# Two row buffers and one scaled-value buffer in decayed attention, and half of the last sums on VectorE

## What is computed

```python
# second layer's attention, 16 query heads, 4 K,V heads, head width 64
q, k, v = x @ Wq.T, x @ Wk.T, x @ Wv.T          # split into heads
q, k = rope(q), rope(k)                          # x * cos + rotate_half(x) * sin
k, v = repeat(k, 4), repeat(v, 4)
# per head with slope s, causal, no softmax:
out[t] = sum over u <= t of exp(-s * (t - u)) * (q[t] . k[u]) * v[u]
x = layernorm(x + out @ Wo.T)
# end of the second layer's feed-forward: every token has two expert answers
x = layernorm(2 * x + answer0 + answer1)         # the kernel's form of it, factors folded in
```

## Time and profile before

| what | value |
|---|---|
| median of 3 runs | 3228.32 us (3227.73 to 3229.99) |
| the profiled execution | 3231.17 us, its span 3229.4 us |
| PE busy | 2767.0 us (86%) |
| DVE busy | 1985.2 us (61%) |
| ACT busy | 1299.3 us (40%) |
| POOL busy | 1068.6 us (33%) |
| granted TensorE clock, mean | 0.942 of full |

### The profile page before, as it was taken

The page is one execution under the profiler, slowest core; times in us unless marked ns, Lnnn a source line. Parts: engine busy times, 40 slices in busy tenths (PEclk is TensorE's granted clock), DMA queues, the critical chain, the costliest instruction groups (busy, mean ns, idle before and its releaser), DMA issues. The chain is left out here.

```text
span 3229.4 us, 62896 instructions
## 1 busy us (share of the span) xinstructions
PE 2767.0 (86%) x17098; PEld 1956.6 (61%) x17099; DVE 1985.2 (61%) x3659; ACT 1299.3 (40%) x2735; POOL 1068.6 (33%) x1446
## 2 busy tenths in 40 slices
PE   6998989999898978877999999969999999809992
PEld 4666666666675647765666666644555555408992
DVE  3656666565666658864555555557777777546664
ACT  2554554545454532212222222215555555424443
POOL 4333343434334311115555555510111111122225
PEclk8999999999999989999999999979999999959996
DMA  2111011111101121112111110022222222052225
GB/s 64 34 31 41 28 38 41 27 38 27 44 24 38 34 80 33 39 70 72 33 32 32 32 32 26 26 67 75 70 65 63 64 64 64 18 172 87 72 74 199
DMA packets 146409, 175.43 MB, mean 54 GB/s; under 512 B 21130, under 2 KB 109730, under 8 KB 145570
## 3 DMA queue, kind: packets, MB, share of 16 engines
q1 hardware_dynamic: 135076, 149.89, 15.9%
q0 software_dynamic: 6912, 18.96, 1.6%
q10 hardware_dynamic: 4224, 4.19, 0.4%
HBM read 90.83 MB, written 37.06 MB: 40 GB/s over the span
## 5 line engine op out<-in xcount | busy, mean ns | idle before, releaser
L560 ACT ACTIVATE soft_probs<-soft_ps_s,soft_mx 128x512 f32<-128x512 f32 x512 | 347.8, 685 | 395.1 <-DVE soft_mx L479 370.4
L479 DVE TENSOR_REDUCE soft_mx<-soft_ps_s 128x1 f32<-128x512 f32 x512 | 329.4, 685 | 236.7 <-PE soft_ps_s L389 224.1
L1817 DVE TENSOR_REDUCE mla_mx<-mla_ps_s 128x1 f32<-128x512 f32 x512 | 334.9, 686 | 133.7 <-PE mla_ps_s L1670 133.2
L1928 ACT ACTIVATE mla_pt<-mla_ps_t 128x512 f32<-128x512 f32 x512 | 289.9, 596 | 265.2 <-PE mla_ps_t L1682 263.1
L389 PE MATMUL soft_ps_s<-soft_ks,soft_qs 128*128 128x512 f32 x1024 | 309.8, 422 | 13.9 <-ACT soft_probs L560 13.9
L398 PE MATMUL soft_ps_p<-ident,soft_probs 128*128 128x128 f32 x2048 | 266.4, 273 | 12.0 <-DVE soft_mx L479 8.5
L398 PEld LDWEIGHTS soft_ps_p<-ident,soft_probs 128*128 128x128 f32 x2048 | 236.7, 141 | 46.7 <-DVE soft_mx L479 10.6
L489 DVE COPY soft_pt<-soft_ps_p 128x512 f32<-128x512 f32 x256 | 175.6, 686 | 138.7 <-PE soft_ps_p L398 134.0
L389 PEld LDWEIGHTS soft_ps_s<-soft_ks,soft_qs 128*128 128x128 f32 x1024 | 171.2, 190 | 147.9 <-issue 59.0
L407 PE MATMUL soft_ps_a<-soft_pt,soft_v 128*64 128x512 f32 x1024 | 251.2, 612 | 0.0
L1670 PE MATMUL mla_ps_s<-mla_stack,mla_pad 128*128 128x512 f32 x512 | 239.4, 474 | 8.8 <-DMA mla_pad<-mla_stack 5.9
(11 more groups left out here) (359 smaller groups left out, 6577.9 us busy)
## 6 DMA issues: line engine op xcount, KB each, us to landing
soft_rrep<-inverse SPq DMA_DIRECT2D x128, 128.0 KB, 2.9
mla_pad<-mla_stack SPq DMA_DIRECT2D x256, 64.0 KB, 2.0
moe_xt<-by_expert SPq DMA_DIRECT2D x72, 129.0 KB, 2.0
soft_ks<-soft_ks SPq DMA_DIRECT2D x64, 128.0 KB, 2.3
decay_ks<-decay_ks SPq DMA_DIRECT2D x64, 128.0 KB, 2.4
raw<-in_L_ffn_w SPq DMA_DIRECT2D x16, 512.0 KB, 5.4
mla_stack<-mla_yh SPq DMA_DIRECT2D x128, 64.0 KB, 2.1
soft_xc<-in_L_attn_x SPq DMA_DIRECT2D x8, 512.0 KB, 4.3
```

The source lines that it names most:

```text
L479: op = vv.tensor_reduce(out=mx[:, h, t:t + 1], in_=ps_s[:, s_bank(4 * h + t), :], axis=AX.X, op=ALU.max, negate=True)
L560: op = nc.scalar.activation(probs[:, h % 2, t, :], ps_s[:, s_bank(4 * h + t), :], ACT.Exp, bias=mx[:, h, t:t + 1], scale=1.0, accum_out=rs ...
L1817: op = vv.tensor_reduce(out=mx[:, a, t, s:s + 1], in_=ps_s[:, (16 * a + 4 * t + s) % S_BANKS, :], axis=AX.X, op=ALU.max, negate=True)
L1928: op = nc.scalar.activation(pt[:, t % 2, s, :], ps_t[:, s % 2, :], ACT.Exp, scale=KPH ** -0.5)
```

## The change

In `decay_attention` the row buffer `rt` becomes two, taken in turn by the units in the order of the products, and `vd` becomes one, so that `VD(g)` waits for `KV2(g-1)`. In `sparse_experts` POOL adds the answers of the even batches only. For an odd batch DVE adds twice the input to the first answer, in place, as soon as the answers are loaded, waits for that, and then adds the second answer. The order on the engines is otherwise as before.

```diff
--- before.py
+++ after.py
@@ -653,13 +653,13 @@
         from_end, to_start = sb("from_end", [P, 2, HEADS]), sb("to_start", [P, PAIRS, CHUNK])
         xc, xb = sb("xc", [P, TT, D]), sb("xb", [P, TT, D])
         xth, xtl = (sb(n, [P, KD, SEQ], F32R) for n in ("xth", "xtl"))
-        rt = sb("rt", [P, 2, HH * HD])
+        rt = sb("rt", [P, 2, 2, HH * HD])
         kr = sb("kr", [P, 2, KVW])
         st = sb("st", [P, 2, HH * 2 * HD])
         qs = sb("qs", [P, HEADS, SEQ], F32R)
         ks = sb("ks", [P, 2, KVH, SEQ], F32R)
         v = sb("v", [P, 2, TT, KVW])
-        vd = sb("vd", [P, 2, 2, GRP * HD])
+        vd = sb("vd", [P, 2, GRP * HD])
         kv = sb("kv", [P, 2, GRP * HD])
         pt = sb("pt", [P, RING, SEQ])
         ot = sb("ot", [P, 2, CHUNK])
@@ -743,7 +743,7 @@
                    "QT": lambda k: (act_s, ("C",) + k), "KT": lambda k: (act_s, ("C",) + k), "W": lambda k: (dve_s, ("F", k[1]))}
         units = [k for k in order["tensor"] if k[0] in ("Q", "KV")]
         st_place = {("HI",) + k: n % 2 for n, k in enumerate(units)}
-        rt_place = {("ROT",) + k: 0 for k in units}
+        rt_place = {("ROT",) + k: n % 2 for n, k in enumerate(units)}
 
         def owner(eng):
             return lambda i, key: shift(i, 1) if key in ahead_keys[eng] else i
@@ -779,7 +779,7 @@
         def rows_of(u):
 
             heads = HH if u[0] == "Q" else KVH
-            line = kr[:, u[1], :] if u[0] == "KV" and u[1] < 2 else rt[:, 0, 0:heads * HD]
+            line = kr[:, u[1], :] if u[0] == "KV" and u[1] < 2 else rt[:, rt_place[("ROT",) + u], 0, 0:heads * HD]
             stack = st[:, st_place[("HI",) + u], 0:heads * 2 * HD]
             return heads, line, line.rearrange("p (h d) -> p h d", d=HD), stack.rearrange("p (h d) -> p h d", d=2 * HD)
 
@@ -913,7 +913,7 @@
                             pe.wait_ge(*pool_s.at(j, "Y1", "KV", 1))
                             for t in range(2):
                                 for s in range(2):
-                                    last = nc.tensor.matmul(m[HD * s:HD * s + HD, 0:GRP * HD], kr[:, t, HD * g:HD * g + HD], vd[:, g % 2, t, :], start=(t == 0), stop=(t == 1))
+                                    last = nc.tensor.matmul(m[HD * s:HD * s + HD, 0:GRP * HD], kr[:, t, HD * g:HD * g + HD], vd[:, t, :], start=(t == 0), stop=(t == 1))
                         elif kind == "IN":
                             g = key[1]
                             pe.wait_ge(*act_s.at(j, "KH", g))
@@ -976,7 +976,7 @@
                             for seq, k in last_use(i, rot, key, rt_place, ahead["vector"], order["vector"]):
                                 dve.wait_ge(*pool_s.at(seq, "LO", *k[1:]))
                             w = heads * HD
-                            op = vv.tensor_tensor(rt[:, :, 0:w].rearrange("p u (h d) -> p u h d", d=HD),
+                            op = vv.tensor_tensor(rt[:, rt_place[key], :, 0:w].rearrange("p u (h d) -> p u h d", d=HD),
                                                   ps_m[:, bank[u], 0:w].rearrange("p (h d) -> p h d", d=HD).unsqueeze(1).broadcast_to([P, 2, heads, HD]),
                                                   rope[:, t, :, :].unsqueeze(2).broadcast_to([P, 2, heads, HD]), ALU.mult)
                         elif kind == "VC":
@@ -988,8 +988,8 @@
                             g = key[1]
                             dve.wait_ge(*pool_s.at(j, "VV", 0))
                             dve.wait_ge(tables_in, 32)
-                            dve.wait_ge(*(pe_s.at(j, "KV2", g - 2) if g >= 2 else pe_s.at(shift(j, -1), "KV2", g + 2)))
-                            op = vv.tensor_tensor(vd[:, g % 2, :, :].rearrange("p t (h d) -> p t h d", d=HD),
+                            dve.wait_ge(*(pe_s.at(j, "KV2", g - 1) if g else pe_s.at(shift(j, -1), "KV2", KVH - 1)))
+                            op = vv.tensor_tensor(vd[:, :, :].rearrange("p t (h d) -> p t h d", d=HD),
                                                   v[:, 1, 0:2, HD * g:HD * g + HD].unsqueeze(2).broadcast_to([P, 2, GRP, HD]),
                                                   from_end[:, :, GRP * g:GRP * g + GRP].unsqueeze(3).broadcast_to([P, 2, GRP, HD]), ALU.mult)
                         elif kind == "M":
@@ -1102,7 +1102,8 @@
                         if kind in ("Y0", "Y1", "HI", "LO"):
                             heads, line, rows, stack = rows_of(u)
                             half = lambda x, c: x.rearrange("p (h c d) -> p h c d", c=2, d=HALF)[:, :, c, :]
-                            a, b = rt[:, 0, 0:heads * HD], rt[:, 1, 0:heads * HD]
+                            place = rt_place[("ROT",) + u]
+                            a, b = rt[:, place, 0, 0:heads * HD], rt[:, place, 1, 0:heads * HD]
                         if kind in ("Y0", "Y1"):
                             c = int(kind[1])
                             hold(pool, *dve_s.at(j, "ROT", *u))
@@ -2283,9 +2284,15 @@
                 for b in range(BATCH):
                     x = b % RAW
                     dve.wait_ge(staged[x], 16 * (len(pieces) // RAW) + 16 * (b // RAW) + 16)
-                    dve.wait_ge(added, b + 1)
-                    vv.scalar_tensor_tensor(out=y_part(b, 1), in0=x_part(b), scalar=2.0, in1=y_part(b, 0), op0=ALU.mult, op1=ALU.add).then_inc(summed, 1)
-                    dve.wait_ge(summed, b + 1)
+                    if b % 2 == 0:
+                        dve.wait_ge(added, b // 2 + 1)
+                        vv.scalar_tensor_tensor(out=y_part(b, 1), in0=x_part(b), scalar=2.0, in1=y_part(b, 0), op0=ALU.mult, op1=ALU.add).then_inc(summed, 2)
+                    else:
+                        dve.wait_ge(tile_in[b], DONE + 32)
+                        vv.scalar_tensor_tensor(out=y_part(b, 0), in0=x_part(b), scalar=2.0, in1=y_part(b, 0), op0=ALU.mult, op1=ALU.add).then_inc(summed, 1)
+                        dve.wait_ge(summed, 2 * b + 1)
+                        vv.tensor_tensor(y_part(b, 1), y_part(b, 0), y_part(b, 1), ALU.add).then_inc(summed, 1)
+                    dve.wait_ge(summed, 2 * b + 2)
                     for t in range(TT):
                         vv.bn_stats(st6[:, b % 2, t, :], y_part(b, 1)[:, D * t:D * t + D]).then_inc(stats, 1)
                     if b >= 2:
@@ -2351,7 +2358,7 @@
 
                 add(0)
                 for b in range(BATCH):
-                    if b + 1 < BATCH:
+                    if b % 2 and b + 1 < BATCH:
                         add(b + 1)
                     hold(pool, means, TT * (b + 1))
                     nc.gpsimd.tensor_scalar(vare[:, b % 2, :, :], mv[:, b % 2, :, 1:2], EPS, None, ALU.add).then_inc(eps_done, 1)
```

## The result

The kernel after takes 3211.71 us, median of seven runs (3204.2 to 3217.9), against 3229.57 us for the kernel before beside it (seven runs, 3227.52 to 3232.81). The ratio is 0.9939 with an interval of 0.9928 to 0.995: faster by 0.5 to 0.7%. The forecast was 3215.2 us. The profiled execution of after is the fastest of its seven, 3204.2 us with a span of 3202.4, so its whole distance to before (27.0 us) isn't what the change is worth; it has to be read stage by stage.

The account below looks back on a forecast made before the run. TensorE's work plus its waits bounds the decayed attention, POOL the last pass. 5.2 + 4.2 + 1.1 + 2.6 = 13.1 us off the profiled 3231.17 gives 3218.1, less 2.85 for the median 3215.2 us; range 3205 to 3223.

Parts of the forecast that it names:

- Part 1: Decayed attention, seven turns: ROT no longer waits for LO, TensorE's 0.83 us mask wait shrinks; 0.74 a turn, 5.2 us.
- The clock: Decayed attention turns: TensorE's clock falls after the long wait; outside the sum, from 6 us lost to some 8 gained.
- rival (c): Decayed attention: TensorE's clock falls less often since shorter waits precede it; 3203 to 3211 us, typically 3208; chance 0.11.
- Part 2: Decayed attention: VD waits for KV2(g-1) instead of KV2(g-2), over 3.3 us before at the tightest place; cost 0.
- Part 3: First pass of the decayed attention: DVE works ahead with two row buffers; 4.2 us saved, ends 2.2 and 5.2.
- The row beside the weight split: First pass: Y0 and Y1 took 3.27 us beside DVE's weight split, so POOL stood still; split's step saves 2.2 us.
- Part 4: Last turn of the decayed attention: TensorE's 1.17 us wait from the last unit's late ROT goes; 1.1 us saved.
- Part 5: Last pass: POOL drops four sums, 9.4 us, but stands still beside DVE; 2.6 us saved, ends -1.0 and +6.3.
- rival (b): Last pass: POOL does not stand still for DVE, the power's 1.75 us has another cause; 3211.5 us; chance 0.05.
- The margin of the transfers: Last pass: batch 5's second part lands by 3202.6, the odd batch's DVE step wants it at 3203.45; margin 0.85 us.
- (a): Decayed attention: first pass and turns hand the time back; 3222 to 3226 us, typically 3225; chance 0.15.
- (d): Decayed attention turns: clock falls longer behind TensorE's 2.12 us wait; 3240 us at three more steps a turn; chance 0.05.

Follow-up runs that it names:

- the two kernels with the masks first: Masks put ahead of all but F in DVE's gap lists, in after and in before: turns 77.95 to 77.98 and 78.83 or 78.84 us.
- mask first: After with masks ahead of all but F in each gap of DVE's list: 3203.55 us in one run, before 3253.67 on that chip.
- the two experiments with its turns: Before with only the single vd: 3231.92 us, ratio 1.0004; before with only the last pass changed: 3227.8 us, ratio 0.9993.
- the PSUM operand: After with the odd batches' addition reading its second operand from PSUM, second expert answer left out: last pass 47.0 us.
- two kernels that pass it: After with all eight last-pass sums on DVE: last pass 47.1 us; after with the odd addition's second operand from PSUM: 47.0 us.
- the four kernels with the masks first: Masks early in DVE's gaps: in after, in before, in after with LA first on POOL, and that with all sums on DVE (ratio 0.9818).
- all sums on DVE: After with all eight batches of the last pass summed on DVE and none on POOL: last pass 47.1 us.
- both first: After with masks early in DVE's gaps and LA first in POOL's: 3197.77 us in one run; with all sums on DVE 3203.66, ratio 0.9818.

## Why the prediction was right

The sign came out as forecast, and the forecast time is 3.5 us above the measured median. The saving was further off, 17.9 us between the medians where 13.1 were figured; the sum started from a median of before that is 1.3 us below the one measured beside after, and that luck hides a part. By its steps, in the profiled execution 18.9 us were saved. The 5.8 us above the sum (stages rounded) are these. With the experiments in place of the two profiles the saving is 14.0 + 3.0 = 17.0 us, so about 2 of the 5.8 us are not the change's.

**Part 1, turns: right in mechanism, the term a little small.** The 0.83 us wait is gone and ROT waits for nothing but TensorE. A turn gained 0.87 us, not 0.74; over six turns that is 0.8 us more. The sum had left 0.1 us of the wait standing, which isn't there, and the step came 0.82 us earlier. At a clock of 1.00 the two kernels with the masks first give the same 0.87.

**The clock: left open, and it gave 2.8 us.** Six turns gained 8.1 us, of which 5.3 are the gain at equal clock; the rest is one long turn instead of two and one turn of 80.10 without a fall. This is rival (c) in small. It was priced by the distance between a long and a short turn (1.2 us); the distance from a short turn to one without a fall is 81.7 - 80.1 = 1.6 us, which no row of before showed. The wait behind which the clock falls was called unchanged, and it was (2.12 and 2.11 us). The step from a wait to the clock was right too, but its size was not seen: mask first took 2.13 us out of a turn at equal clock and another 1.6 us of clock out of a usual one. How much of the 2.8 is the change's stays open. Before's second long turn was chance, 1.2 us, since the two experiments with its turns have one; the turn of 80.10 has its like in two of the three other profiles with after's decayed attention, and in none of the three with before's.

**Part 2, the buffer of scaled values: right.** 1.0004 as a ratio alone, and the same 0.5 us wait for VD with one buffer and with two once it shows at all.

**Part 3, the first pass: 5.3 for 4.2, of which 0.4 is not the change's.** From the first XH on it is 4.9 us (62.80 and 57.94 us), inside the ends of 2.2 and 5.2; what lies ahead of the first XH took 3.64 to 5.45 us in the twelve profiles. The row beside the weight split was misread: not both Y's were held. In after Y0 began 0.68 us ahead of the split (1456.09 against 1456.77) and took 0.73 us, as long as it does alone. Only Y1 was held; it took 2.86 us and ended 0.57 us behind the split. The working put both behind the split, at little cost: LO ended at 1461.95, where the working, counted from the first XH, gives 1462.20. KV2(0) came 3.8 us earlier instead of 3.3. The remaining 1.1 us come near the end of the pass, where 0.9 were figured: the wait of 0.76 for LO is 0.22 now, the one of 1.02 for a mask 0.67.

**Part 4 and the seventh turn: 2.4 for 1.8.** The wait of the earlier trace rows is gone, and so is one of 0.23 us behind it (before 2098.00) that the sum didn't count: 1.40, and with the turn's 0.87 some 2.3. At equal clock the two kernels with mask first differ by 2.65.

**Part 5, the last pass: 3.1 for 2.6, and the queue ran as written.** Counted from the end A of the even batch's aggregation (3160.12, where L2292 can start at 3160.18), EPS ends at A+1.37 (forecast 1.3), the power at A+3.46 (3.44), the sum of the next even batch at A+6.6 (6.6), its power at A+8.86 (8.8), and the next A follows after 9.58 (9.67). Three pairs of 0.09 are 0.3 us of the difference. Another 0.14 is that A of before had been put 0.14 us late, at 3184.10: the four aggregations overlap, and the next instruction of DVE begins 0.33 us behind the first of them (3160.18 against 3159.85), less than their busy time of 0.41. One sign was off: powers of 1.7 us and more are six of eight, not seven, and the one of batch 3 took 1.44 us. That GpSimd stands still while DVE reads two SBUF operands was the premise; the PSUM operand shows it, 1.06 against 1.90 us, and so rival (b) is out. The rule that was named beside it, the shared port pair of "SBUF — State Buffer" in the Trainium skill, section "Who interferes with whom", holds here in both cases tried (held with two SBUF inputs, free with one). The "DVE-end + ~115 ns" of the same page stands there for a transfer that GpSimd issues beside a DVE copy. It fits EPS, which ends 0.08 us after L2292, and not the power, which ends 0.92 us after L2294: a step that needs 1.04 us by itself isn't over when DVE lets go. The margin of the transfers was put at 0.85 us; two kernels that pass it gain 0.4 and 0.5 us.

**Rivals.** (a) didn't happen: nothing was handed back. (d) didn't happen: of the six turns one is long, where before had two. Its place was well chosen all the same, since without that wait the clock fell in no turn.

What stays open: the clock's state after the 2.1 us wait differs from turn to turn with the same work ahead of it (0.53, 1.00, 1.00 in the third stretch of 2 us behind XH in the first three turns of after, of which the second fell one stretch later, to 0.61), and nothing in these runs says which turn gets which.

## What to carry to other kernels

A buffer that is written once per unit and read by a slower engine costs time where something urgent is queued behind its writer, so look for these places one by one. Here the second buffer was worth 0.9 us a turn even after the urgent step had been moved away, since the writer itself is awaited. Where three queues run strictly in order, the cheapest edit is the order: masks that TensorE waits for ahead of copies that it doesn't yet need brought 31 us here, twice what the buffer did. And a wait of TensorE should be priced with what its clock does behind it: of the 3.7 us that the masks' new place took out of a usual turn, 1.6 us were waiting and 1.6 us were the clock.

## What the runs showed of the hardware

A turn has three lengths by the granted clock and by nothing else: 80.10 at 1.00, 81.7 at 0.98 and 83.04 us at 0.96 in after, with 498 matmuls and 5.82 us of TensorE idle in each. With TensorE fed through the two stretches behind XH (2.00 and 1.49 us of work in 2 us each) the clock stayed at 1.00 in all 24 turns of the four kernels with the masks first.

A GpSimd step that is held by a DVE step with two SBUF inputs ends at DVE's end plus its own length alone, less 0.12 to 0.15 us. Four lengths show it: EPS (0.23 us alone) ends 0.08 us behind DVE, Y1 (0.72) 0.57, the power (1.04) 0.90 to 0.92, and the sum of two answers (2.34) 2.19, in these rows of before:

```profile
3181.11 1.23 DVE L2287 SCALAR_TENSOR_TENSOR moe_w1l<-raw,moe_w1h 128x1024 f32<-128x1024 f32 x1 [11.37 <-POOL moe_w1h L2350]
3181.68 2.85 POOL L2350 TENSOR_TENSOR moe_w1h<-moe_w1h,moe_w1l 128x1024 f32<-128x1024 f32 x1 [0.68 <-DMA moe_w1l<-answers]
```

The latent attention, which none of these kernels edits, took 621 to 625 us in every profile of the first chips and 640 to 656 us in the six profiles on the later ones; before, run beside those, was 24 and 32 us slower as well. TensorE's waits for ScalarE and for the padded stack's transfers are longer in the first of these (16.7 us in all sums on DVE against 10.9 in after, and 8.5 against 5.5), which explains only a part. One thing stands in all six profiles on the later chips and in none of the six on the first ones: idle stretches of DVE and ScalarE that end with a release which the profile calls "remote", up to 6.6 us long and on DVE 11 to 27 us in all. TensorE stands still with them (3.91 us at 2326.73 in both first). What releases them isn't shown. A few microseconds may also come from what precedes the stage; the runs can't tell this from the chip. It is why whole times from different chips are not set beside each other here.
